# Constant 128x128 matmuls into an unread PSUM bank, in three places of a two-attention and expert-layer kernel

## The chip, the cores and the metric

The kernel runs on one core of one Trainium2 chip. A core has TensorE (PE, matmuls; its weight loads are listed as PEld), VectorE (DVE), ScalarE (ACT), GpSimd (POOL) and SyncE (SP, which here issues most of the DMAs). The metric is the device time of one execution in microseconds, lower is better. The time before is the median of three runs.

## The reference

```python
x = x + layernorm(linear_attention(layernorm(x)))   # x: (2, 1024, 256), 16 heads, chunks of 64
x = x + layernorm(ffn(layernorm(x)))

def ffn(x):
    h = x + attention(rmsnorm(x, ln1_w))   # 32 heads, 8 key/value heads, head size 64, causal
    return h + moe(rmsnorm(h, ln2_w))      # 8 experts, hidden size 1024, top 2

def moe(t):
    probs = softmax(t @ gate_w)
    topw, topi = top_k(probs, 2)
    # each token: weighted sum over its two experts of (relu(t @ w1) * (t @ w3)) @ w2
```

## The kernel before

Each engine has its own program, written out by hand, and the engines meet at semaphores (`wait_ge`). PE works strictly in its written order, so a PE instruction placed before a `wait_ge` is executed while PE would otherwise wait there. Everything is float32 unless a shape says bf16 or fp32r. A float32 matmul appears in the trace as two MATMUL records, a transpose as one.

The program has these stages.

- **First loads.** SP and ACT issue the loads of the weights and of `x`. POOL writes the constants (`ident`, `tri`, masks). PE transposes two weights (L1117) when the load of `wo` has landed, multiplies the small parameters once (L1120), and then folds the feature weights (L1141), with the first transposes of the normalised `x` in the middle (`turn_xn(0)`, L1126).
- **Linear attention.** `pair_step(s, ...)` runs for s = 0 to TB + 2 = 10, with TB = 8 pairs of 128-token tiles. Step s works on the front of pair s, the middle of pair s - 1 and the end of pair s - 3. At s = 9 and 10 only ends of pairs are left: a wait for `r_ready`, then four transposes (`turn(bank[1], ...)`, L1126). At s = 8 the first projections of the softmax attention are made (`project`, L1292), at s = 9 the first four scores (`score(0, h)`, L1326 and L1327), of which h = 3 waits for `v2_ready`.
- **Softmax attention.** 128 tiles (`for t in range(TILES + 2)`): scores, transposed probabilities (L1343), weighted values (L1355), output projection (L1364). Between the two attentions PE waits for the layer norms of the last pair, a chain of small DVE, POOL and ACT operations that ends in `r_ready`.
- **Router.** PE transposes `h` (L1395) and multiplies it by the gate (L1402, 64 records of 8 columns). DVE takes the softmax, the two best experts and their places. PE is asked for two small products in between (L1406 and L1407, after `router_steps`), for 32 bf16 products that find the token of each slot (L1413, in four groups that follow `inplace_ready`), and for 32 that find its weight (L1417, after `worth_ready` 2).
- **Expert slots.** 39 slots of 128 rows, three at a time: one transpose of the rows (`turn_slot`, L1425), 32 matmuls of w1 and w3 (L1441), eight of w2 (L1450). SP loads the expert weights, and the first nine loads of 1 MB start during the router.
- **The end.** The sums come back from memory, are normalised and stored. PE has nothing there.

PSUM has eight banks: `bank[0]` to `bank[3]` and the four of `wide`. `bank[3]` holds nothing that is still to be read in the places of the change.

Of the kernel before, what the change touches and what calls it, by code (L numbers as in the profile page):

```python
# [14 lines left out]
P = 128  # L15
# [4 lines left out]
TB = SEQ // P  # L20
# [61 lines left out]
def place_in_half(n, half):  # L82

    return 2 * HALF if half else n % 2 * HALF


def build(nc, a, out):
    ctx = ExitStack()
    with ctx:
        def sb(name, shape, dt=F32):  # L90
            return ctx.enter_context(nc.sbuf_tensor(name, shape, dt))
# [12 lines left out]
        def score_bank(t, h):  # L104

            if t % TB < TB // 2:
                return wide[:, h, :]
            return wide[:, 2 * (h % 2):2 * (h % 2) + 2, :].rearrange("p a b -> p (a b)")
# [15 lines left out]
        def S(name):  # L124

            if name not in sems:
                sems[name] = ctx.enter_context(nc.semaphore(name))
            return sems[name]


        bank = [ctx.enter_context(nc.psum_tensor(f"bank{i}", [P, 512], F32)) for i in range(4)]
# [6 lines left out]
        wo2 = sb("wo2", [P, NKV, 2, D])  # L138

        ident = sb("ident", [P, P])  # L140
        tri = sb("tri", [P, P])
        headmask = sb("headmask", [P, HB])
        rowmask = sb("rowmask", [P, HR])
# [246 lines left out]

        @block.gpsimd
        def _(gp):
            nc.gpsimd.memset(ident[:], 0.0).then_inc(S("constants_ready"), 1)
            nc.gpsimd.memset(tri[:], 1.0).then_inc(S("constants_ready"), 1)
            nc.gpsimd.memset(headmask[:], 1.0).then_inc(S("constants_ready"), 1)
# [712 lines left out]
        @block.tensor  # L1108
        def _(pe):
            mm = nc.tensor.matmul  # L1110
            pe.wait_ge(S("constants_ready"), NCONST)

            pe.wait_ge(S("wnat_loaded"), 64)
# [8 lines left out]
            def turn(to, src, given):  # L1122

                for k in range(KB):
                    for b in range(BATCH):
                        ins = nc.tensor.transpose(to[:, (k * BATCH + b) * P:(k * BATCH + b + 1) * P], src(k, b), ident[:])  # L1126
                ins.then_inc(S(given), 1)

            def turn_xn(s):
                pe.wait_ge(S("xn_ready"), s + 1)  # L1130
                if s:
                    pe.wait_ge(S("v_ready"), s)
                turn(bank[3], lambda k, b: xn[:, b, k * P:(k + 1) * P], "xnT_psum")
# [13 lines left out]
            def pair_step(s, front, mid, last):  # L1147
# [39 lines left out]
                    output(0)  # L1187
                if front and s:
                    turn_xn(s)
                if last:  # L1190
                    pe.wait_ge(S("r_ready"), s - 2)
                    if s <= TB:
                        pe.wait_ge(S("ktok_ready"), s)
                    turn(bank[1], lambda k, b: rn[:, b, k * P:(k + 1) * P], "rT_psum")
                if s == TB + 1:
                    for h in range(G):
                        score(0, h)
# [97 lines left out]
            def scores_read(t, h):  # L1295

                ct = t % TB
                if ct == 0:
                    return G * (t - 1) + 3 + h // 2
                if ct < TB // 2:  # L1300
                    return G * (t - 1) + h + 1
                if ct == TB // 2 and h < 2:
                    return G * (t - 1) + 2 * h + 2
                return G * t + h - 1

            def score(t, h):
                n, ct = divmod(t, TB)
                if ct == 0 and h == 0:
                    pe.wait_ge(S("k_doubled"), n * 2 + 1)
                    pe.wait_ge(S("qlo_ready"), n * 4 + 1)  # L1310
                if ct == 0 and h == 2:
                    pe.wait_ge(S("qlo_ready"), n * 4 + 2)
                if t == 0 and h == 3:
                    pe.wait_ge(S("v2_ready"), 1)
                if ct == TB // 2 and h == 0:
                    pe.wait_ge(S("k_doubled"), n * 2 + 2)
                    pe.wait_ge(S("qlo_ready"), n * 4 + 4)
                if t:
                    pe.wait_ge(S("nmax_ready"), scores_read(t, h))
                w = (ct + 1) * P  # L1320
                at = place_in_half(n, ct >= TB // 2) + ct % (TB // 2) * P
                q = qhl[:, h, at:at + P]
                for half in range(1 if w <= HALF else 2):
                    lo, cols = place_in_half(n, half), min(w - half * HALF, HALF)
                    dst = score_bank(t, h)[:, half * HALF:half * HALF + cols]
                    mm(dst, q, khi[:, lo:lo + cols], start=True, stop=False)  # L1326
                    ins = mm(dst, q, klo[:, lo:lo + cols], start=False, stop=True)  # L1327
                ins.then_inc(S("scores2"), 1)

            for s in range(TB + 3):  # L1330
                pair_step(s, s < TB, 1 <= s <= TB, s >= 3)
# [35 lines left out]
            for t in range(TILES + 2):  # L1367
                scored, turning, weighing = t < TILES, 1 <= t <= TILES, t >= 2
                if scored and t:
                    score(t, 0)  # L1370
                if weighing:
                    values(t - 2)
                if scored and t:
                    score(t, 1)
                if turning:
                    turn_part(t - 1, 0)
                if scored and t:
                    score(t, 2)
                if turning:
                    turn_part(t - 1, 1)  # L1380
                if weighing:
                    project_out(t - 2)
                if scored and t:
                    score(t, 3)
                if turning:
                    turn_part(t - 1, 2)
                if scored and item_of(t):
                    project(item_of(t))
# [13 lines left out]
                    ins = mm(wide[:, 0, i * E:(i + 1) * E], hT[:, k, i * P:(i + 1) * P], gate[:, k], start=(k == 0), stop=(k == KB - 1))  # L1402
            ins.then_inc(S("logits_psum"), 1)

            pe.wait_ge(S("router_steps"), ROUTED)
            mm(bank[0][:, 0:E * NT], tri[:], picked[:].rearrange("p e t -> p (e t)"), start=True, stop=True)  # L1406
            mm(bank[1][:, 0:E * NT], ones[:], picked[:].rearrange("p e t -> p (e t)"), start=True, stop=True).then_inc(S("ranks_psum"), 1)  # L1407


            pe.wait_ge(S("worth_ready"), 1)  # L1410
            for c in range(C):
                pe.wait_ge(S("inplace_ready"), c * 4 // C + 1)
                ins = mm(bank[2][:, 0:2 * NS], inplace[:, c], worth[:, c, 0:2].rearrange("p v s -> p (v s)"), start=(c == 0), stop=(c == C - 1))  # L1413
            ins.then_inc(S("found_psum"), 1)
            pe.wait_ge(S("worth_ready"), 2)
            for c in range(C):
                ins = mm(bank[1][:, 0:3 * NS], inplace[:, c], worth[:, c, 2:5].rearrange("p v s -> p (v s)"), start=(c == 0), stop=(c == C - 1))  # L1417
# [11 lines left out]
            with pe.Fori(0, NS // UR) as it:  # L1429
                for u in range(UR):  # L1430
# [3 lines left out]
                    for half in range(2):  # L1434
                        for at, w, name in ((0, "w1", "up_psum"), (2, "w3", "gate_psum")):
# [3 lines left out]
                            for f in range(4):  # L1439
                                for k in range(KB):  # L1440
                                    ins = mm(wide[:, at + half, f * P:(f + 1) * P], w[:, k, (half * 4 + f) * P:(half * 4 + f + 1) * P], sT[u][:, k],  # L1441
                                             start=(k == 0), stop=(k == KB - 1))
# [31 lines left out]
```

## Time and profile before

| | |
|---|---|
| runs before | 1832.23, 1832.38, 1833.19 us; median 1832.38 us |
| profiled execution: span | 1831.4 us |
| median less the profiled span | 0.98 us |
| PE busy | 1742.7 us, 95% of the span |
| PE weight loads | 1387.1 us, 76% |
| DVE, ACT, POOL busy | 1036.2, 1059.7 and 207.9 us |
| mean granted TensorE clock | 0.976 |

The profiled execution has no time of its own beside its span, from its first to its last instruction. Times in the rows are microseconds from the start of the span. The granted clock is a share of full speed: 1.00 is 2.4 GHz and 0.50 is 1.2 GHz. A time in brackets at the end of a row is how long that engine had been idle before it, with what released it.

### The profile page before, as it was taken

What the parts mean: (1) busy time and instruction counts of PE and PEld (TensorE: products, weight loads), DVE (VectorE), ACT (ScalarE), POOL (GpSimd) and SP (SyncE); (2) the same over time, 40 slices, a digit from 0 to 9 for tenths busy, and PEclk for the clock granted to TensorE, in tenths of its full rate; (3) what the DMA queues carried; (4) which work ended last, traced back from release to release, by engine and by line L of the source; (5) the groups of instructions that cost most, each with busy time, mean ns of one, the idle gap of its engine ahead of it and who ended that gap; (6) DMA issues with size and microseconds to landing.
All of it is one profiled execution on the core that took longest, in us unless ns stands there. A gap on an engine that the chain in (4) does not pass through costs nothing.

```text
span 1831.4 us, 31651 instructions
## 1 busy us (share of the span) xinstructions
PE 1742.7 (95%) x12158; PEld 1387.1 (76%) x12158; DVE 1036.2 (57%) x2595; ACT 1059.7 (58%) x2376; POOL 207.9 (11%) x236
## 2 busy tenths in 40 slices
PE   7999799999999999999999999999939999999993
PEld 6777477777777777777777777777739999999993
DVE  3777667777677677686686677676661111111112
ACT  3344677777777787787777787777731222222223
POOL 2223100000000000000000000000011222222222
PEclk9999899999999999999999999999968999999997
DMA  3000100000000000000000000000053153113533
GB/s 87 1 2 2 47 1 10 1 1 10 1 1 10 1 1 10 1 1 10 1 1 10 1 1 1 1 1 24 1 193 112 23 160 92 29 23 92 153 102 97
DMA packets 46102, 60.17 MB, mean 33 GB/s; under 512 B 8993, under 2 KB 39585, under 8 KB 45985
## 3 DMA queue, kind: packets, MB, share of 16 engines
q1 hardware_dynamic: 35088, 46.15, 7.5%
q0 software_dynamic: 7536, 10.36, 3.4%
q10 hardware_dynamic: 3360, 2.10, 0.4%
q8 instruction: 73, 1.20, 0.3%
q14 instruction: 45, 0.36, 0.1%
HBM read 138.43 MB, written 11.40 MB: 82 GB/s over the span
## 4 chain that ended last, share of the span: by engine, by line
PE 93%; DVE 3%; ACT 1%; POOL 1%; DMA 1%; issue 1%; ACTq 0%; POOLq 0%; DVEq 0%
PE wide L1441 15%; PE bank L1355 14%; PE bank L1343 14%; PE wide L1326 9%; PE bank L1292 9%; PE wide L1327 8%; PE bank L1450 7%; PE bank L1364 6%; PE bank L1153 3%; PE wide L1165 1%; PE bank L1239 1%; PE bank L1178 1%; PE bank L1228 1%; PE bank L1282 1%; PE bank L1126 1%
## 5 line engine op out<-in xcount | busy, mean ns | idle before, releaser
L921 DVE CUSTOM_DVE_ANT_0 arena<-wide,arena 128x896 f32<-128x896 f32 (+7 forms) x512 | 382.9, 755 | 249.3 <-PE wide L1327 243.1
L671 ACT ACTIVATE arena<-arena,nmax 128x896 f32<-128x896 f32 (+7 forms) x512 | 399.1, 780 | 90.0 <-DVE nmax L921 87.8
L683 ACT COPY arena<-bank 128x512 f32<-128x512 f32 x576 | 311.5, 586 | 82.7 <-PE bank L1343 77.1
L1326 PE MATMUL wide<-khi,qhl 128*128 128x512 f32 (+3 forms) x768 | 345.2, 450 | 1.4 <-DVE vt L905 1.3
L1343 PE MATMUL bank<-ident,arena 128*128 128x128 f32 x2304 | 309.4, 274 | 1.7 <-DVE arena L929 0.5
L1441 PEld LDWEIGHTS wide<-wo,arena 128*128 128x128 f32 x2496 | 286.9, 193 | 3.3 <-issue 1.4
L1441 PE MATMUL wide<-wo,arena 128*128 128x128 f32 x2496 | 287.3, 276 | 1.0 <-ACT wo L727 1.0
L1343 PEld LDWEIGHTS bank<-ident,arena 128*128 128x128 f32 x2304 | 260.0, 141 | 28.6 <-issue 13.4
L1355 PE MATMUL bank<-arena,vt 128*64 128x256 f32 x2304 | 276.9, 385 | 0.0
L929 DVE TENSOR_SCALAR arena<-arena,rinv 128x896 f32<-128x896 f32 (+7 forms) x512 | 257.8, 525 | 9.1
L1085 DVE TENSOR_TENSOR wo<-wide,wo 128x512 f32<-128x512 f32 x78 | 53.9, 691 | 368.2 <-PE wide L1441 368.2
L1327 PE MATMUL wide<-klo,qhl 128*128 128x512 f32 (+3 forms) x768 | 256.7, 347 | 0.0
L1355 PEld LDWEIGHTS bank<-arena,vt 128*64 128x64 f32 x2304 | 154.1, 136 | 90.9 <-issue 19.5
L1326 PEld LDWEIGHTS wide<-khi,qhl 128*128 128x128 f32 x768 | 145.3, 189 | 89.2 <-issue 58.7
L1327 PEld LDWEIGHTS wide<-klo,qhl 128*128 128x128 f32 x768 | 146.0, 190 | 37.4 <-issue 22.5
L737 ACT ACTIVATE wo<-wide 128x512 f32<-128x512 f32 x78 | 46.6, 597 | 170.4 <-PE wide L1441 170.4
L1450 PE MATMUL bank<-arena,wo 128*128 128x256 f32 x624 | 141.1, 379 | 0.0
L1364 PE MATMUL bank<-wo,oT 128*128 128x256 f32 x512 | 134.4, 385 | 0.9 <-ACT oT L693 0.9
L479 POOL CAST khi<-khi 64x512 fp32r<-64x512 f32 x32 | 19.5, 608 | 979.2 <-ACT khi L661 979.1
L1450 PEld LDWEIGHTS bank<-arena,wo 128*128 128x128 f32 x624 | 115.5, 190 | 14.1
L1292 PE MATMUL bank<-rT_all,wq_g 128*128 128x512 f32 x248 | 116.7, 593 | 0.0
L671 ACT ACTIVATION_READ_ACCUMULATOR arena<-arena,nmax 128x1 f32 x512 | 99.0, 193 | 0.0
(232 smaller groups left out, 1569.3 us busy)
## 6 DMA issues: line engine op xcount, KB each, us to landing
arena<-in_L_ffn_w SPq DMA_DIRECT2D x117, 1024.0 KB
wq_g<-in_L_ffn_wq SPq DMA_DIRECT2D x8, 256.0 KB, 3.0
wo<-in_L_ffn_wo SPq DMA_DIRECT2D x16, 128.0 KB, 3.1
hbuf<-acc SPq DMA_DIRECT2D x2, 1024.0 KB, 4.5
tbuf<-rT_all SPq DMA_DIRECT2D x4, 512.0 KB, 3.0
acc<-hbuf SPq DMA_DIRECT2D x4, 512.0 KB, 5.9
out<-x_all SPq DMA_DIRECT2D x8, 256.0 KB, 2.1
x_all<-in_L_attn_x ACTq DMA_DIRECT2D x2, 896.0 KB, 9.1
```

The lines of the kernel that those rows point to most:

```text
L671: nc.scalar.activation(probs[t % 2][:, h, 0:w], probs[t % 2][:, h, 0:w], ACT.Exp, bias=nmax[:, t % 2, h:h + 1], scale=-1.0, accum_out=rsum ...
L683: nc.scalar.copy(pT[t % 2][m], bank_of((t, m))).then_inc(S("pT_ready"), 1)
L921: nc.vector.tensor_tensor_reduce(out=probs[t % 2][:, h, 0:w], in0=score_bank(t, h)[:, 0:w], in1=causal[:, SEQ - w:SEQ], scale=-1.0, scalar ...
L929: nc.vector.tensor_scalar(probs[t % 2][:, h, 0:w], probs[t % 2][:, h, 0:w], rinv[:, t % 2, h:h + 1], None, ALU.mult).then_inc(S("probs_rea ...
L1292: ins = mm(to, w, rT_all[:, k, at:at + HALF], start=(k == 0), stop=(k == KB - 1))
L1326: mm(dst, q, khi[:, lo:lo + cols], start=True, stop=False)
L1327: ins = mm(dst, q, klo[:, lo:lo + cols], start=False, stop=True)
L1343: ins = nc.tensor.transpose(to[:, h * P:(h + 1) * P], probs[t % 2][:, h, m * P:(m + 1) * P], ident[:])
L1355: ins = mm(bank[2][u * DH:(u + 1) * DH, 0:2 * P], vt[:, n % 2, m], pT[t % 2][m][:, u * 2 * P:(u + 1) * 2 * P], start=(m == 0), stop=(m == ct))
L1364: ins = mm(bank[2][:, 2 * P:2 * P + D], oT[:, j], wo2[:, t // (BATCH * TB), j], start=(j == 0), stop=(j == 1))
L1441: ins = mm(wide[:, at + half, f * P:(f + 1) * P], w[:, k, (half * 4 + f) * P:(half * 4 + f + 1) * P], sT[u][:, k], start=(k == 0), stop=(k ...
L1450: ins = mm(bank[u][:, 0:D], gated[:, f], w2_e[u][:, f], start=(f == 0), stop=(f == FB - 1))
```

## The change

A tile `busywork` of 128x128 ones is written by POOL as its first constant. `keep_busy(n)` issues n float32 matmuls of that tile with itself into the first 128 columns of `bank[3]`, each a complete group of its own. Nothing reads the result, and no semaphore is raised by it. It stands in seven spots of PE's program.

```diff
+        busywork = sb("busywork", [P, P])
...
         def _(gp):
+            nc.gpsimd.memset(busywork[:], 1.0).then_inc(S("busywork_ready"), 1)
             nc.gpsimd.memset(ident[:], 0.0).then_inc(S("constants_ready"), 1)
...
             mm = nc.tensor.matmul
+
+            def keep_busy(times):
+
+                for _ in range(times):
+                    mm(bank[3][:, 0:P], busywork[:], busywork[:], start=True, stop=True)
+
+            pe.wait_ge(S("busywork_ready"), 1)
+            keep_busy(14)
             pe.wait_ge(S("constants_ready"), NCONST)
...
+                if s > TB:
+                    keep_busy(6 if s == TB + 1 else 22)
                 if last:
                     pe.wait_ge(S("r_ready"), s - 2)
...
                 if t == 0 and h == 3:
+                    keep_busy(5)
                     pe.wait_ge(S("v2_ready"), 1)
...
             ins.then_inc(S("logits_psum"), 1)
 
+            keep_busy(20)
             pe.wait_ge(S("router_steps"), ROUTED)
...
+            keep_busy(42)
             pe.wait_ge(S("worth_ready"), 1)
...
             ins.then_inc(S("found_psum"), 1)
+            keep_busy(26)
             pe.wait_ge(S("worth_ready"), 2)
```

## Rows read from the trace of the kernel before

**Rows 1.** The page, part 2: PE's granted clock in 40 slices.
```profile
PEclk9999899999999999999999999999968999999997
```

**Rows 2.** Windows, PE alone: stretch, length, PE busy (records), granted clock, DMA share, GB/s.
```profile
13.00:16.00 3.00, 3.00 (x15) 1.00 1.11 367
18.00:19.00 1.00, 1.00 (x11) 1.00 0.00 0
30.70:33.18 2.48, 0.00 (x1) 1.00 0.00 0
185.31:188.50 3.19, 1.51 (x11) 1.00 0.38 98
200.00:205.57 5.57, 5.57 (x13) 0.50 0.00 0
1333.25:1338.79 5.54, 5.54 (x53) 1.00 0.09 27
1378.59:1383.16 4.57, 4.57 (x21) 0.50 1.03 388
```

**Rows 3.** Timeline, first 11 us: start, length, instruction, idle before.
```profile
0.78 0.20 POOL L393 MEMSET ident<- 128x128 f32 x1 [0.29 <-POOLq L1464]
...
7.85 1.94 PE L1117 MATMUL bank<-ident,arena 128*128 128x128 f32 x8 [7.85 <-DMA arena<-in_L_attn_wo]
...
10.80 0.69 PE L1120 MATMUL bank<-small,rep 16*128 16x69 f32 x2 [1.01 <-DMA small<-in_L_attn_norm_w]
```

**Rows 4.** Chain that ended last, merged, first 20 us: start, length, work.
```profile
12.73 3.78 PE wide L1141 x16
16.51 0.85 PE bank L1126 x4
17.37 2.07 PE wide L1141 x16
```

**Rows 5.** Timeline, PE between the two attentions.
```profile
178.93 3.60 PE L1292 MATMUL wide<-rT_all,wq_g 128*128 128x512 f32 x8
...
183.32 1.99 PE L1239 MATMUL bank<-arena,wo 128*128 128x256 f32 x8 [0.41 <-DVE wo L868]
...
186.82 0.66 PE L1126 MATMUL bank<-ident,arena 128*128 128x128 f32 x4 [1.51 <-ACT arena L649]
...
189.68 0.47 PE L1326 MATMUL wide<-khi,qhl 128*128 128x128 f32 x1 [1.28 <-DVE vt L905]
...
197.86 1.12 PE L1126 MATMUL bank<-ident,arena 128*128 128x128 f32 x4 [7.50 <-ACT arena L649]
...
200.00 3.75 PE L1292 MATMUL bank<-rT_all,wkv_g 128*128 128x512 f32 x4 [1.02 <-ACT rT_all L586]
```

**Rows 6.** Timeline, PE in the router, with the DVE row that reads the logits.
```profile
1333.25 8.61 PE L1402 MATMUL wide<-gate,arena 128*128 128x8 f32 x64
...
1343.26 0.29 DVE L983 TENSOR_TENSOR glog<-wide,hrstd 128x128 f32<-128x128 f32 x1 [3.07 <-POOL hrstd L442]
...
1350.86 0.79 PE L1406 MATMUL bank<-picked,tri 128*128 128x128 f32 x2 [9.01 <-DVE picked L1004]
...
1363.46 0.68 PE L1413 MATMUL bank<-worth,inplace 128*128 128x78 bf16 x8 [11.38 <-DVE inplace L1055]
...
1366.78 0.70 PE L1413 MATMUL bank<-worth,inplace 128*128 128x78 bf16 x8 [0.43 <-DVE inplace L1055]
...
1373.85 3.33 PE L1417 MATMUL bank<-worth,inplace 128*128 128x117 bf16 x32 [6.37 <-DVE worth L1071]
1376.97 0.64 PE L1425 MATMUL bank<-ident,wo 128*128 128x128 f32 x2
...
1378.59 9.58 PE L1441 MATMUL wide<-wo,arena 128*128 128x128 f32 x64 [0.97 <-ACT wo L727]
...
1388.00 0.38 PE L1425 MATMUL bank<-ident,wo 128*128 128x128 f32 x2
```

**Rows 7.** Chain that ended last, merged, second expert slot.
```profile
1391.84 7.14 PE wide L1441 x64
```

## The prediction

> **What bounds the kernel now.** I read the clock row of the page first: 36 of the 40 slices stand at 9, the others are slice 5, slices 30 and 31 around the router, and the last, where PE has no work [rows 1]. PE is busy for 95% of the span (the table above), so its speed sets nearly all of the time, and the only thing that matmuls without a reader can change is the speed of the others. So the next view is the windows around the dips, for when the clock falls and rises and what PE had done before, and then the timeline and the chain of waits, for which PE work at the low clock lies on the path.
>
> The clock rises under unbroken work: 5.57 us after L1292 begins at 200.00, and 4.57 us after L1441 begins at 1378.59 [rows 2, 5, 6]. It falls in two ways. At 188.50 it falls 3.19 us after L1239 has ended (183.32 + 1.99 = 185.31), although 1.51 us of that stretch held short PE work [rows 2, 5]. At 1338.79 it falls while PE is fully busy, under the 8-column records of L1402 [rows 2, 6]. A stretch of 2.48 us with no PE work (30.70 to 33.18) did not make it fall [rows 2].
>
> The first microseconds need a second look. The granted clock is shown as 1.00 from the start, but 15 records of L1141 pass in the 3.00 us from 13.00, and 11 in the 1.00 us from 18.00 [rows 2]. The first 16 take 3.78 us in the chain, the last 16 take 2.07 [rows 4]. Full speed for this shape is 7.14 / 64 = 0.112 us a record [rows 7], half speed twice that, 0.223. So PE ran at half speed until x of the last 16 records had passed, with 0.223x + 0.112(16 - x) = 2.07, x about 2.5: until about 17.9, again some 5.2 us after unbroken work began at 12.73. The page "TensorE: Matmul & The Clock Gate" of the Trainium skill (Part 1, HAM trace caveats) says that recorded clock events have been unreliable; here the record counts decide, and they agree that the first value is not to be believed.
>
> **The filler's size.** One filler matmul is two records of 128 columns, the shape of L1441: 0.223 us at the high clock and 0.446 at the low one. Below each block stands in the idle time that covers it.
> - 14 matmuls: PE starts near 1.0, when a memset like L393 (0.78 + 0.20) is done. Wholly at half speed they take 6.2 us, to 7.2; L1117 starts at 7.85 for its load [rows 3]. Covered by 0.6 us.
> - 6: 1.34 us from 185.31, at the high clock; the next work starts at 186.82 [rows 5]. Covered.
> - 5: 1.12 us, in the 1.28 us before 189.68 [rows 5]. Covered.
> - 22: from about 190.1. High clock 4.9 us, to 195.0; low clock 9.8, to 199.9. L1126 starts at 197.86 [rows 5]. Covered at the high clock.
> - 20: from 1333.25 + 8.61 = 1341.86, low clock throughout 8.9 us, to 1350.8; L1406 starts at 1350.86 [rows 6]. Covered. The logits are not late either: their reader L983 waits for POOL [rows 6].
> - 42: from about 1351.5; 9.4 us high, 18.7 low. The first L1413 starts at 1363.46, the fourth group only at 1366.78 [rows 6].
> - 26: from about 1367.1; 5.8 us high, 11.6 low. L1417 starts at 1373.85 [rows 6], so 6.4 us are free.
>
> The POOL memset delays the other constants by about the 0.15 us at which such memsets follow one another (L393 lasts 0.20); PE needs them at 7.85, when it waits for the load, so I cost it at nothing, and 0.2 us if that cover were gone. No transfer is moved. The fetching of some 540 more PE instructions, and the filler's reads beside DVE's, have no row. The nearest are the 64 records of L1441 in 7.14 us, unrolled and beside working engines [rows 7], which are at the full rate, so the cost is 0; the other bound is the filler's smallest cover, 0.1 us at the 20, overrun by as much again in each of five blocks, 0.5. I take 0.
>
> **What the clock does in each place, and what that is worth.**
>
> Place 1, first loads. The filler ends by 7.2, or up to 1 us earlier if the clock rises near its end. Then until 12.73 PE has only L1117 and L1120, 2.6 us at half speed and less at full [rows 3]. That is a gap of 5.5 us or more with little in it, and such a gap made the clock fall at 188.50 after 3.19 us. So I expect a rise near 6, a fall before 12.73 and L1141 as before. Left is L1120, 0.69 us at half speed; by the L1425 pair, 0.64 against 0.38 [rows 6], it saves 0.2. Upper bound, if the clock stays up: 36 records from 12.73 in 36 x 0.112 = 4.0 instead of 3.78 + 0.85 + 2.07 = 6.7 [rows 4], so 2.5 with the last wait of each piece, and 2.7 with L1120. Lower bound 0. I take 0.2.
>
> Place 2, between the attentions. With 6 and 5 in the gaps PE has no 3 us without dense work around 188.50, so that fall is gone. The 22 end at about 195.0 at the high clock. From there to about 199.6 there are only the four transposes of L1126: again more than 3.19 us with little work. I expect the fall to come there, about 198.5 to 200. L1126 then runs at the high clock, 0.66 instead of 1.12 [rows 5]: 0.46 saved. L1292 and the first scores stay at the low clock for a time like the 5.57 us before. Upper bound, if it stays up: L1126 0.46, L1292 3.75 - 1.80 = 1.9 (four records of the eight in 3.60) [rows 5], and half of the 1.8 us from 203.75 to 205.57, 0.9: 3.2. Lower bound 0 (a fall before 197.86). I take 0.5.
>
> Place 3, router. The 20 start at the low clock; after about 5 us it rises, near 1347. L1406 and L1407, the same four records as L1126 in count and columns, then save 0.46 (1.12 - 0.66) [rows 5], and the whole DVE chain moves up by that. The 42 run at the high clock to about 1361, and are covered in any case where at most about 7 us of them are low (9.4 + 7/2 = 12.9 us, to 1364.5, and PE catches up before the fourth group). From 1361 to 1366.6 PE has only L1413, 0.68 us of work in each 1.1 us, so the clock falls again, and the 26 start low at 1367.0. With a rise after 5.1 us (the mean of 4.57 and 5.57) 23 of their 52 records are slow: 5.1 + 29 x 0.112 = 8.35 us, to 1375.4, where 1373.4 would have done. That is 2.0 us late. But L1417 then takes 3.33 / 2 = 1.67, ending at 1377.1 against 1377.2, and L1425 saves 0.2, so L1441 starts 0.3 earlier. L1441 is then at the high clock from the beginning and saves half of 4.57 [rows 2], 2.3. Sum 2.6. Upper bound, if the clock stays up all through: 0.46 + 0.35 (half of the last L1413 group's 0.70) + 1.67 + 0.2 + 2.3 = 5.0. Lower bound 1.9, a rise 1.4 us later in the 26.
>
> Sum: 0.2 + 0.5 + 2.6 = 3.3 us. Against the profiled span this is 1831.4 - 3.3 = 1828.1, and with the 0.98 us between the median and that span **1829.1 us**, 0.18% below the median.
>
> **The rivals.**
>
> A is this case: the filler buys the clock, but the gaps it does not fill give it back twice, and it pays at L1441. Its own range is 1827.0 to 1830.8: the moments of fall and rise can shift by some 2 us in each place, each worth half, as the 4.57 against 5.57 shows.
>
> B: the clock stays up through the gaps that are left, because a few microseconds with some work in them are not enough once the work before was dense (30.70 to 33.18 had none and no fall [rows 2]). Then 2.7 + 3.2 + 5.0 = 10.9 us, 1821.5. Against it stands 188.50. The page "TensorE: Matmul & The Clock Gate" (HAM oscillation) describes a kernel that waits for data between bursts of matmuls and starts every burst slow again; by that rule B falls out and the sum is A's 3.3 us. The trace agrees at 188.50, 3.19 us after dense work.
>
> C: nothing moves. The falls come in the gaps anyway, the late 26 eat the rest: 1832.4, within 0.5 us.
>
> D: slower. The filler itself stands in the way, because the clock does not rise under it. The 42 then end at 1352.1 + 18.7 = 1370.8, the 32 L1413 records (0.70 / 8 each) at 1373.6 instead of 1367.5, 6.1 us late. The 6.37 us from there to L1417 [rows 6] bring 1380.0, but the 26 end at 1385.2: 11.4 us late in all. The 22 add 199.9 - 197.86 = 2.0. Sum 13.4, 1845.8. It decides only if the 42 spend more than 7 us at the low clock. Against it: L1441 is the same shape, and under it the clock rose in 4.57 us [rows 2].
>
> **How the numbers follow.** A 0.58, B 0.22, C 0.11, D 0.09. The bound of 0.2% is 3.7 us, about what a measurement of this kernel can tell from no change: below 1828.7 is faster, above 1836.0 slower. A lies on both sides of 1828.7, some 0.45 of it below (0.26). Faster: 0.26 + 0.22 = 0.48. Same: 0.32 + 0.11 = 0.43. Slower: 0.09. The range reaches from B's 1821.5 to 1833.5, which holds A and C and leaves out D and the far side of B; the likeliest case's own range is the 1827.0 to 1830.8 above.
>
> **What would show it.** Right: granted clock at 1.00 under L1406; a fall between 1361 and 1367; L1417 near 1.7 us and starting about 1375.4, released by no other engine; L1441 at 64 records in about 7.2 us. Between the attentions no fall at 188.5 but one near 199, and L1292 still near 3.7 us. At the start, L1141's 16 records still at 3.8 us. Wrong: L1292 at 1.8 us or the first L1141 block under 2.5 us (B), or a filler block over 9 us long that ends after the wait behind it (D).

## The result: 1829.77 us, 0.16% less

The changed kernel's median is 1829.77 us (1828.2 to 1831.16, 11 runs) against 1832.23 us of the kernel before in the same session (11 runs). The ratio is 0.9984, 95% interval 0.9976 to 0.9992: 2.5 us less, with an interval of 1.5 to 4.4 us. The prediction was 1829.1, a gain of 3.3 us, by case A. The profiled execution spans 1829.4 us, the one before 1831.4; it took 1831.14 us, 1.4 above the median and second slowest of its eleven.

The page of the changed kernel, parts 1 and 2, the clock row against [rows 1]:

```profile
PE 1777.3 (97%) x12428; PEld 1422.3 (78%) x12428; DVE 1036.5 (57%) x2595; ACT 1059.7 (58%) x2376; POOL 208.1 (11%) x237
...
PEclk9999999999999999999999999999979999999997
```

PE has 270 more matmul records and is 35 us busier, and the kernel is faster: the dip at slice 5 is gone, one of the two around the router is nearly gone. Windows of the changed kernel, PE alone, with the columns of [rows 2]:

```profile
12.35:15.92 3.57, 3.57 (x17) 0.50 1.02 338
...
194.70:197.40 2.70, 0.00 (x0) 1.00 0.67 201
197.48:198.10 0.62, 0.62 (x4) 1.00 0.32 109
199.16:205.10 5.94, 5.94 (x15) 0.50 0.00 0
...
1335.40:1343.60 8.20, 8.20 (x40) 0.50 0.01 3
...
1366.20:1367.40 1.20, 0.77 (x13) 0.50 1.14 365
1367.41:1372.40 4.99, 4.99 (x27) 0.50 1.02 404
1373.00:1375.70 2.70, 2.70 (x26) 1.00 1.10 354
1378.68:1386.00 7.32, 7.32 (x65) 1.00 0.93 335
```

Each place shows the same picture: the clock is up at the latest behind a filler block, and down again after the next gap. The first filler is at half speed nearly to its end (28 records in 6.30 us, 0.225 each), and the transposes behind it run high (L1127, 1.07 us instead of 1.94). The filler of 20 is at the low clock until 1348.5 at least. The clock is down at 12.35 although the first filler had ended at 7.34, down at 199.16 after the gap of 2.80 us before the transposes, and down at 1366.20 after the 78-column products. Only the last filler is followed by dense work, and there the clock stays. The timeline of the changed kernel, PE alone, answers to [rows 3, 5, 6]; L1117 is now the filler, L1127 was L1117, L1130 was L1120, L1151 was L1141, L1163 (the features) was L1153, L1136 was L1126, L1304 was L1292, L1415 was L1402, L1428 and L1433 were L1413 and L1417, L1457 was L1441, L1466 was L1450:

```profile
1.04 6.30 PE L1117 MATMUL bank<-busywork 128*128 128x128 f32 x28 [1.04 <-POOL busywork L394]
8.01 1.07 PE L1127 MATMUL bank<-ident,arena 128*128 128x128 f32 x8 [0.67 <-DMA arena<-in_L_attn_wo]
10.48 0.62 PE L1130 MATMUL bank<-small,rep 16*128 16x69 f32 x2 [1.40 <-DMA small<-in_L_attn_norm_w]
12.35 3.78 PE L1151 MATMUL wide<-fdiagT,arena 128*128 128x128 f32 x16 [1.24 <-DVE fdiagT L794]
...
18.87 5.34 PE L1163 MATMUL bank<-arena 128*128 128x256 f32 x24
...
189.56 5.13 PE L1117 MATMUL bank<-busywork 128*128 128x128 f32 x44
197.48 0.65 PE L1136 MATMUL bank<-ident,arena 128*128 128x128 f32 x4 [2.80 <-ACT arena L651]
199.16 3.75 PE L1304 MATMUL bank<-rT_all,wkv_g 128*128 128x512 f32 x4 [1.02 <-ACT rT_all L588]
...
1332.42 11.35 PE L1415 MATMUL wide<-gate,arena 128*128 128x8 f32 x64
1343.62 7.08 PE L1117 MATMUL bank<-busywork 128*128 128x128 f32 x40
...
1363.59 0.45 PE L1428 MATMUL bank<-worth,inplace 128*128 128x78 bf16 x8 [2.03 <-DVE inplace L1057]
...
1367.41 8.47 PE L1117 MATMUL bank<-busywork 128*128 128x128 f32 x52
1375.72 1.83 PE L1433 MATMUL bank<-worth,inplace 128*128 128x117 bf16 x32
...
1378.68 7.41 PE L1457 MATMUL wide<-wo,arena 128*128 128x128 f32 x64 [0.90 <-ACT wo L729]
...
1386.14 3.62 PE L1466 MATMUL bank<-arena,wo 128*128 128x256 f32 x16
```

The row to stop at is L1415. The gate block took 8.61 us before and takes 11.35 here, with nothing changed in it. DVE's reader of the logits, which before had waited for POOL [rows 6], now waited for PE. Timeline of the changed kernel, DVE:

```profile
1343.87 0.29 DVE L985 TENSOR_TENSOR glog<-wide,hrstd 128x128 f32<-128x128 f32 x1 [4.52 <-PE wide L1415]
```

The router's gain and loss, from the start of the gate block to the start of w2's block (L1450: 1333.25 to 1388.22 before, 1332.42 to 1386.14 after), add up as follows.

| piece | before | after | change |
|---|---|---|---|
| gate block start to the reader of the logits | 10.01 | 11.45 | +1.44 |
| reader to the first small product | 7.60 | 7.60 | 0 |
| small products to the first 78-column group | 12.60 | 12.12 | -0.48 |
| first group to the start of the last 32 products | 10.39 | 12.13 | +1.74 |
| last 32 products to the start of w1 and w3 | 4.74 | 2.96 | -1.78 |
| w1 and w3 of the first slot | 9.63 | 7.46 | -2.17 |
| sum | 54.97 | 53.72 | -1.25 |

### The profile page after: what moved, and what is told of

It is laid out like the page before. It is cut to its first block, busy times and chain, and to the rows that moved or that the text cites. A ratio compares the mean times of both kernels' runs of the same rounds, so it can differ in the third digit from the quotient of the medians.

```text
span 1829.4 us, 32192 instructions
## 1 busy us (share of the span) xinstructions
PE 1777.3 (97%) x12428; PEld 1422.3 (78%) x12428; DVE 1036.5 (57%) x2595; ACT 1059.7 (58%) x2376; POOL 208.1 (11%) x237
## 3 DMA queue, kind: packets, MB, share of 16 engines
q8 instruction: 76, 1.25, 0.3%
## 4 chain that ended last, share of the span: by engine, by line
PE 94%; DVE 3%; ACT 1%; POOL 1%; DMA 1%; issue 0%; ACTq 0%; POOLq 0%; DVEq 0%
PE wide L1457 15%; PE bank L1368 14%; PE bank L1356 14%; PE wide L1339 9%; PE bank L1304 9%; PE wide L1340 8%; PE bank L1466 7%; PE bank L1377 6%; PE bank L1163 3%; PE wide L1175 1%; PE bank L1251 1%; PE bank L1188 1%; PE bank L1240 1%; PE bank L1294 1%; PE wide L1415 1%; PE bank L1136 1%
## 5 line engine op out<-in xcount | busy, mean ns | idle before, releaser
L1457 PEld LDWEIGHTS wide<-wo,arena 128*128 128x128 f32 x2496 | 284.8, 192 | 3.1 <-issue 1.1
L1457 PE MATMUL wide<-wo,arena 128*128 128x128 f32 x2496 | 285.1, 275 | 0.9 <-ACT wo L729 0.9
L1466 PE MATMUL bank<-arena,wo 128*128 128x256 f32 x624 | 141.1, 379 | 0.0
L1466 PEld LDWEIGHTS bank<-arena,wo 128*128 128x128 f32 x624 | 115.5, 190 | 14.1
L1304 PE MATMUL bank<-rT_all,wq_g 128*128 128x512 f32 x248 | 116.7, 593 | 0.0
```

Of the source, the lines that this page charges most:

```text
L1304: ins = mm(to, w, rT_all[:, k, at:at + HALF], start=(k == 0), stop=(k == KB - 1))
L1466: ins = mm(bank[u][:, 0:D], gated[:, f], w2_e[u][:, f], start=(f == 0), stop=(f == FB - 1))
```

## The experiments

Twelve runs follow, eleven other kernels and the changed one again. All medians are set against the kernel before on the same chip in the same session (1832.47 us in the first session, 1833.53 in the second, 1832.21 in the third). The ratios differ by up to 0.0007 (1.3 us) from the quotients of the medians shown, which is inside their intervals. Where the median's interval of about 0.1% (1.7 us) is too wide for the question, pieces of the timeline bounded by the same two instructions are compared. They belong to one execution each, and agree to 0.1 us only where the clock rose and fell at the same places in both.

### Each place alone

`p1_only` keeps only the 14 matmuls, `p2_only` only the 6, 5 and 22, `p3_only` only the 20, 42 and 26, and `only_26` only the last block. The edit of `p3_only` against the changed kernel:

```diff
-            keep_busy(14)
...
-                if s > TB:
-                    keep_busy(6 if s == TB + 1 else 22)
...
-                    keep_busy(5)
```

> Only the 14 matmuls in the first loads are kept. Theory (the clock is bought and given back in the gap behind): the clock rises near 7.6 us and falls near 11, the first 16 records of the feature fold L1141 of before still take 3.8 us, and the time is that of before less 0 to 0.4 us. Rival (the clock stays up): those 16 records take under 2.3 us and the time falls by 2.5 us or more.

Measured: 1832.34 us, ratio 0.9998 (0.9989 to 1.0007). Timeline of this kernel, PE:

```profile
1.04 5.26 PE L1117 MATMUL bank<-busywork 128*128 128x128 f32 x28 [1.04 <-POOL busywork L394]
...
12.80 3.78 PE L1151 MATMUL wide<-fdiagT,arena 128*128 128x128 f32 x16 [1.24 <-DVE fdiagT L794]
```

28 records in 5.26 us instead of 6.2 show that the clock rose inside the filler, near 5.3 by an estimate from the two rates (0.223 and 0.112 us a record) and not near 7.6 as expected, and L1151 at 3.78 us shows that it was down again. The first block buys nothing by itself that the median can tell.

> Only the 6, 5 and 22 matmuls between the attentions are kept. Theory: no fall at 188.5, one near 199, the four transposes of the last pair at 0.65 us, the projections behind them still 3.75 us; time 0.4 to 0.8 us less than before. Rival (the clock stays up until the attention): projections at 1.8 us and 3 us less.

Measured: 1832.38 us, ratio 0.9998 (0.9989 to 1.0007). Timeline, PE:

```profile
197.54 0.66 PE L1135 MATMUL bank<-ident,arena 128*128 128x128 f32 x4 [2.80 <-ACT arena L651]
199.22 3.75 PE L1303 MATMUL bank<-rT_all,wkv_g 128*128 128x512 f32 x4 [1.02 <-ACT rT_all L588]
...
1332.39 11.08 PE L1414 MATMUL wide<-gate,arena 128*128 128x8 f32 x64
```

The transposes take 0.66 us and the projections 3.75, as the theory has it. From the transposes of the pair before (186.48) to the projections (199.22) it is 12.74 us, against 200.00 - 186.82 = 13.18 before [rows 5]: 0.44 gained, too little for the median. The gate block took 11.08 us here although nothing of the change is in the router, and 11.39 in `p1_only`. So the fillers of the router are not what lengthens it.

> Only the 20, 42 and 26 matmuls of the router are kept. Theory: the expert slots' first w1 and w3 block runs at the high clock and the time is 2.3 to 2.8 us less than before, provided that the 64 gate records end before POOL's hrstd, as before. Rival (the late gate records of the changed kernel come from the change itself, not from when the clock falls): the gate block takes 11.3 us again and only 1.2 us are gained.

Measured: 1830.95 us, ratio 0.9988 (0.9979 to 0.9997). The gate block took 10.47 us, with its reader again released by PE. From its start to the w2 block 1386.00 - 1333.90 = 52.1 us, 2.9 less than the 54.97 before and 3.8 less than the 55.89 of `p1_only` and `p2_only`, whose router holds no filler and whose gate block was long (1333.70 to 1389.59, 1332.39 to 1388.28). The theory's size is met in the piece, though its condition was not. The median shows 1.5 us of it. In this execution 1.6 us were lost elsewhere, in the linear attention, where this kernel has no filler (see the last section). The rival (a long gate block only with the change) falls with the two runs above.

> Only the last block of 26 is kept. Theory (the 42 buy nothing, since the clock falls again under the 78-column products, and the 20 buy 0.46 us): the 26 start at the low clock and end some 2 us after the weights of DVE are ready, L1441 of before runs at the high clock from its first record; time 1.8 to 2.3 us less than before, at most 0.5 us slower than with all three blocks of the router. Rival (all three are needed): under 1 us gained.

Measured: 1831.09 us, ratio 0.9989 (0.998 to 0.9998). Timeline, PE:

```profile
1333.08 8.53 PE L1411 MATMUL wide<-gate,arena 128*128 128x8 f32 x64
...
1367.12 7.15 PE L1117 MATMUL bank<-busywork 128*128 128x128 f32 x52
1374.12 1.83 PE L1427 MATMUL bank<-worth,inplace 128*128 128x117 bf16 x32
...
1377.08 7.41 PE L1451 MATMUL wide<-wo,arena 128*128 128x128 f32 x64 [0.90 <-ACT wo L729]
```

The gate block is short here, 8.53 us. One block of 26 gives what all three of the router give, within 0.2 us of median and so within the intervals. All three places together gain 2.5 us; alone they gain 0.1, 0.1 and 1.5, sums that agree within the intervals.

### Without the 42, and fewer than 26

```diff
-            keep_busy(42)
```

> The changed kernel without the block of 42. Theory (the clock falls again behind it anyway): the time within 0.5 us of the changed kernel's. Rival (the 42 are what keeps the clock up until the slots): 1.5 us or more slower.

Measured: 1829.08 us, ratio 0.9981 (0.9972 to 0.999), beside 1829.53 for the changed kernel. The 42 buy nothing that the median can tell. The other edit:

```diff
-            keep_busy(26)
+            keep_busy(19)
```

> The changed kernel with 19 instead of 26 matmuls in the last block. Theory (the block starts low and ends 1.5 to 2 us late; 14 records at the high clock are worth 1.6 us): the block ends at 1373.5 to 1374.5 and the time falls by 0.5 to 1.5 us. Rival (a shorter block no longer raises the clock before L1441 of before): the time rises by 0.5 to 2 us.

Measured: 1829.49 us, ratio 0.9981 (0.9972 to 0.999), no difference from the changed kernel's 1829.53. In the timeline the block ends earlier: from the first 78-column group to the last 32 products 1374.28 - 1363.54 = 10.74 us against 1375.91 - 1364.14 = 11.77 in the changed kernel beside it, 1.0 less, and L1457 still takes 7.41 us. The gate block took 11.17 us in the one and 10.08 in the other, so the executions do not agree where they should. The lateness is real in the piece. The forecast gain of 0.5 to 1.5 us is not in the median, and what the lateness is worth there is not settled.

> The changed kernel itself, beside the three others on one chip. Theory: 1829.8, and the moments of fall and rise shifted against the first profile by up to 3 us, by the start of the execution. Rival: none; it is the measure for the others.

Measured: 1829.53 us (1828.38 to 1831.32), ratio 0.9984 (0.9975 to 0.9993), the first result again. Its gate block took 10.08 us, against 11.35 in the first profile of the same kernel, and its last filler 8.12. From the gate block to the w2 block it is 1386.34 - 1334.24 = 52.1 us, 2.9 less than before.

### Narrow filler: 8 columns instead of 128

```diff
-                    mm(bank[3][:, 0:P], busywork[:], busywork[:], start=True, stop=True)
+                    mm(bank[3][:, 0:8], busywork[:], busywork[:, 0:8], start=True, stop=True)
```

> The changed kernel with every filler product 8 columns wide instead of 128, the same count of instructions in the same places. Theory (it is the wide products that hold and raise the clock, as the 8-column gate records lost it while PE was fully busy): clock as in the kernel before, low under L1441 of before for 4 to 5 us, and the time of before within 1 us (1831.5 to 1833.5). Rival (any unbroken issue of matmuls raises the clock, or the gain has another cause): a time within 1 us of the changed kernel's 1829.8, and a rise during the filler.

Measured: 1841.38 us, ratio 1.005 (1.0036 to 1.0063): 9 us slower than before by the ratio and by the profiled spans (1840.4 against 1831.4), 8 by the medians. Timeline, PE:

```profile
1335.63 8.73 PE L1415 MATMUL wide<-gate,arena 128*128 128x8 f32 x64
...
1354.26 17.93 PE L1117 MATMUL bank<-busywork 128*128 128x8 f32 x84
...
1374.08 11.24 PE L1117 MATMUL bank<-busywork 128*128 128x8 f32 x52
1385.17 3.31 PE L1433 MATMUL bank<-worth,inplace 128*128 128x117 bf16 x32
...
1389.81 7.41 PE L1457 MATMUL wide<-wo,arena 128*128 128x128 f32 x64 [0.90 <-ACT wo L729]
```

The clock side of the theory holds for the filler: 84 records take 17.93 us, 0.213 each, so none of them ran at the high clock, and PE was fully busy. The rival falls. It does not hold behind it: L1457 was forecast low for 4 to 5 us and took 7.41 us, all at the high clock, which rose near 1388.8, 3.7 us after the last 32 products had begun. Before, the same products (from 1373.85) did not bring the rise until 1383.16; there PE had been idle for 6.37 us ahead of them, here it had been busy. Which difference did it is open. So this kernel has the saving at L1457 too, and loses by lateness. The time was forecast wrong: I had taken the narrow products for cheap, and at the low clock they take as long as wide ones. The run is therefore case D of the prediction as it would look: the last 32 products start at 1385.17 where before it was 1373.85, 11.3 us later, of which 2.4 were lost before the gate block (1335.63 against 1333.25).

### The gaps closed

`fill12` closes the gaps of the first two places:

```diff
-            keep_busy(14)
+            keep_busy(15)
...
                 ins.then_inc(S("wT_psum"), 1)
+            keep_busy(5)
             pe.wait_ge(S("small_loaded"), 16 * 9)
...
+            keep_busy(5)
             pe.wait_ge(S("fdiag_ready"), 1)
...
-                    keep_busy(6 if s == TB + 1 else 22)
+                    keep_busy(6 if s == TB + 1 else 33)
...
+            keep_busy(4)
             pe.wait_ge(S("rT_ready"), TB)
```

> The changed kernel with the gaps of the first two places closed: 15 instead of 14 at the start, 5 more matmuls in each of the two waits before the feature fold L1141 of before, 33 instead of 22 before the last transposes and 4 behind them. Theory (the gaps give the clock back): no fall between about 7 us and the gate, the first fold block in under 2.3 us, the projections in 1.9 us; 5 us less than the changed kernel's time in sum (2.5 in each place), at least 3.5 us. Rival (the gaps are not the cause, or the filler delays the work behind it): under 1.5 us less, or slower.

Measured: 1825.1 us, ratio 0.9959 (0.9945 to 0.9973). Timeline, PE:

```profile
10.15 0.43 PE L1131 MATMUL bank<-small,rep 16*128 16x69 f32 x2 [0.19 <-DMA small<-in_L_attn_norm_w]
10.51 1.38 PE L1117 MATMUL bank<-busywork 128*128 128x128 f32 x10
11.82 2.05 PE L1153 MATMUL wide<-fdiagT,arena 128*128 128x128 f32 x16
...
15.94 6.42 PE L1165 MATMUL bank<-arena 128*128 128x256 f32 x29
...
194.53 0.66 PE L1137 MATMUL bank<-ident,arena 128*128 128x128 f32 x4 [0.34 <-ACT arena L651]
...
196.20 1.96 PE L1306 MATMUL bank<-rT_all,wkv_g 128*128 128x512 f32 x4
```

The fold takes 2.05 us instead of 3.78, the projections 1.96 instead of 3.75. From the small product to the features it is 15.94 - 10.15 = 5.79 us, against 18.87 - 10.48 = 8.39 in the changed kernel: 2.6 gained, where the prediction's upper bound for place 1 was 2.7. Place 2 gave less than the 2.5 us forecast: from the transposes of the pair before to the gate block it is 1327.67 - 183.48 = 1144.19 us against 1332.42 - 186.42 = 1146.00, 1.8 gained. From its ratio to the changed kernel's it is 0.9959 against 0.9984, 4.6 us. The granted clock is 1.00 throughout 6 to 26 us and 184 to 204 us. The gap behind the filler was the cause.

`fill3` closes the gap around the 78-column products:

```diff
-            keep_busy(42)
+            keep_busy(49)
...
             for c in range(C):
+                if c and c % (C // 4) == 0:
+                    keep_busy(2)
                 pe.wait_ge(S("inplace_ready"), c * 4 // C + 1)
```

> The changed kernel with the gap around the 78-column products closed: 49 instead of 42 before them and 2 matmuls between each two of their four groups. Theory: no fall near 1366, the 26 take 5.8 us instead of 8.5 and PE is idle before the last 32 bf16 products; 1.5 to 2.0 us less than the changed kernel. Rival (the 26's lateness is covered anyway by the gather of the rows): under 0.5 us less.

Measured: 1828.08 us, ratio 0.9972 (0.9963 to 0.9982), 1.7 us below the changed kernel's 1829.77 of the first result, or 2.2 by the ratios. Timeline, PE:

```profile
1365.85 0.46 PE L1430 MATMUL bank<-worth,inplace 128*128 128x78 bf16 x8 [0.15 <-DVE inplace L1057]
1366.15 6.04 PE L1117 MATMUL bank<-busywork 128*128 128x128 f32 x52
1372.68 1.84 PE L1435 MATMUL bank<-worth,inplace 128*128 128x117 bf16 x32 [0.49 <-DVE worth L1073]
```

The same 52 records take 6.04 us instead of 8.47, and PE waits for DVE again before L1435. From the first 78-column group to the last 32 products it is 1372.68 - 1362.54 = 10.14 us, against 12.13 in the changed kernel and 10.39 before: the 1.7 us lost to the late filler are back in the piece.

> The gaps of all three places closed (the edits of the two filled kernels together; the gate block untouched). Theory (each gap gives back its own part, and they add): 5 us from the first two places and 1.8 from the router below the changed kernel, 1823.0, granted clock high except for some 10 us under and behind the gate block. Rival (the parts share a cover, or the longer filler delays the work behind it): no faster than with the first two places closed, 1825.1.

Measured: 1824.53 us (1824.3 to 1824.88, 5 runs), ratio 0.9955 (0.9941 to 0.9969). It is the fastest kernel of the study, 5.0 us below the changed kernel beside it (1829.53) and 0.45% below the one before. In the router, from gate block to w2 block, it takes 1379.72 - 1329.40 = 50.3 us against 52.5 in `fill12` (1327.67 to 1380.13), 2.1 less; of the medians 0.6 is left of that, inside the intervals. The forecast 1823.0 was missed, and the median lies nearer to the rival's 1825.1. The two profiles show where most of the rest went, and it is not in the places of the change. The clock fell at the end of the linear attention's 2.5 us gap in this execution and not in that of `fill12`, and from the work behind the gap (L1177) to the next L1165 it took 35.55 - 30.21 = 5.34 us against 33.84 - 29.84 = 4.00. So the parts add in the pieces, and the medians do not show it.

### A filler inside the gate block

```diff
+                if i >= 4:
+                    mm(wide[:, 1, 0:P], busywork[:], busywork[:], start=True, stop=True)
...
-            keep_busy(20)
+            keep_busy(32)
```

> The changed kernel with one filler matmul before the gate products of each of the last 12 tiles, and 32 instead of 20 behind them. Theory (the 8-column records lose the clock, and in executions where it falls early they make the logits late): if one filler in each 0.64 us is enough to hold the clock, the gate block takes 9.5 us, the logits are not late and the time is 0.5 to 1.5 us less than the changed kernel's. Rival (the clock falls nevertheless): gate block over 14 us, the router late by 3 to 8 us.

Measured: 1835.46 us, ratio 1.0013 (1.0004 to 1.0022), slower than before and 5.7 us slower than the changed kernel. Timeline, PE, the gate records behind the second and behind the last of the twelve:

```profile
1334.75 0.51 PE L1417 MATMUL wide<-gate,arena 128*128 128x8 f32 x4
...
1347.07 0.86 PE L1417 MATMUL wide<-gate,arena 128*128 128x8 f32 x4
1347.78 9.56 PE L1117 MATMUL bank<-busywork 128*128 128x128 f32 x64
1357.18 0.39 PE L1422 MATMUL bank<-picked,tri 128*128 128x128 f32 x2
```

Four gate records take 0.51 us early and 0.86 later: the clock fell all the same, and then each filler cost the logits about twice its price (two records in 0.77 us instead of 0.47). The block lasted from 1332.07 to 1347.8, and the 32 behind it held up the small products too. The rival held.

## Why the prediction was right, and where it was off

- **What the clock does in each place.** Right in all three, as case A had it, but for the moment of the first rise. Place 1: the rise, forecast near 6, came when the filler was all but over (7.34); fall before 12.35, the fold at 3.78 us. Place 2: no fall at 188.5, a fall between 198.1 and 199.16 (forecast 198.5 to 200), the transposes 0.65, the projections 3.75. Place 3: high clock under the small products, low at 1366.20 (forecast a fall between 1361 and 1367), the last 32 products starting at 1375.72 (forecast 1375.4) in 1.83 us (1.7), w1 and w3 in 7.41 us (7.2).
- **Place 1, 0.2 us.** It was 0.08: 8.39 from the small product to the features against 19.27 - 10.80 = 8.47 before. The start was another 0.3 us early, because the work on the small parameters, released by the load of `norm_w`, began at 10.48 and not 10.80; in `p2_only`, with no filler there, it was 10.25, so this looks like scatter.
- **Place 2, 0.5 us.** It was 0.44: from the transposes of the pair before to the projections 199.16 - 186.42 = 12.74 us, against 13.18. The terms of its upper bound add up to 3.3 and not 3.2, which changes nothing.
- **Place 3, 2.6 us.** It was 1.25 between the profiles. The step that was off is the sentence that the logits are not late. It rested on one execution in which the clock fell 5.5 us into the gate block; in the profile after it fell about 2.5 us into it (the stretch from 1332.58 to 1335.30 has a mean of 0.94, the next one 0.50), the block took 11.35 us and the logits came 1.4 us late. Without this the place is 1.25 + 1.44 = 2.7 us, the forecast, and in `changed_again`, where the logits were only 0.2 us late, it was 2.9. The fall came early in `p1_only` and `p2_only` too, and the same kernel had a gate block of 11.35 and of 10.08 us, so the loss goes with the execution. That the kernel before pays it in some executions too is likely but not shown, as it has only one profile.
- **How near the sum came.** The forecast gain was 3.3 us, the median's is 2.5, the profiles' 2.0. The pieces of the profiles add up: 0.08 + 0.3 + 0.44 + 1.25 = 2.1. The 0.98 us added at the end is no constant of the measurement. It says that the profiled execution before was slower than its median, and so was the one of the changed kernel: there the median less the span is 0.37. That 1829.1 lies 0.7 from the median, while the forecast span, 1828.1, lies 1.3 from the measured one, is in part luck.
- **Rivals.** B fell as a forecast of this kernel, but its bounds were fair prices. With the gaps closed place 1 gave 8.47 - 5.79 = 2.7 of 2.7, place 2 2.2 of 3.2 (1146.43 from 186.82 to the gate block before, less 1144.19), and the router 54.97 - 50.32 = 4.65 of 5.0. The kernel with all gaps closed gained 7.7 of B's 10.9 us. C fell by the interval, which excludes 1. D was seen in `narrow` and, in part, in `gate_fill`. Its condition, that the 42 spend more than 7 us at the low clock, was not met by wide products: the 42 ran high from the start (84 records in 9.54 us).
- **The page cited against B.** The page "TensorE: Matmul & The Clock Gate" of the Trainium skill (HAM oscillation) describes a kernel that waits between bursts and starts each burst slow. The runs agree with it: 12.35, 199.16 and 1366.20 are such starts (the last after sparse work and not after a bare wait), and with the waits filled they are gone.

## What to carry to other kernels

In this kernel a filler matmul paid only for dense work that follows it at once; look at the gap behind it before sizing it, and fill that gap or leave the filler out. Size it by both clocks: a block that starts low takes up to twice its length, and what stands over the wait is paid in full. Fillers must not stand in front of or among narrow products that are near the path, and narrow products are no filler.

## What the runs showed of the hardware that was not expected

- **The moment of fall and rise is not set by the kernel's work alone.** The same gate block, untouched, took between 8.53 and 11.39 us in thirteen profiled executions, by when the clock fell in it. Behind the linear attention's 2.5 us gap the clock did not fall in [rows 2], but it did in four others (`p3_only`, `narrow`, `changed_again`, `fill123`): at the end of the gap in `fill123`, 1.3 to 1.6 us later in the other three. The work behind the gap ran low and lost 1.3 to 1.6 us. `p3_only` has no filler ahead of it, and the same kernel as `changed_again` was without this fall in its first profile, so this too goes with the execution. In `fill3` the clock fell under the dense fold itself, near 13.2, and those 16 records took 2.92 us instead of 3.78. Windows of `p3_only`, PE alone, the last row being that of `fill123`:

```profile
33.60:34.20 0.60, 0.60 (x16) 0.50 0.00 0
34.50:36.80 2.30, 2.30 (x37) 0.50 0.00 0
...
30.20:33.30 3.10, 3.09 (x37) 0.50 0.00 0
```

- **An 8-column float32 record costs as much as a 128-column one at the low clock**: 28 in 6.14 us in `narrow`, 28 in 6.30 in the changed kernel. What sets this was not tried; each record brings its own 128-column weight load.
- **A fully busy PE can hold the low clock for long**: 84 narrow records in 17.93 us without a rise.
